# Layer-norm statistics by ScalarE passes, register loads in three parts, and another order in the set-up, in a one-core image kernel

## The reference

```python
x = x + warp(x, fside, angle)            # rigid transform, bilinear gather from the image itself
x = x + ffn(x, expert)                   # relu(x wi^T + low-rank parts) wo^T + low-rank parts,
                                         # low-rank: common ones and those of one of 8 experts per image
x = x + pool(x, prompt)                  # scores tanh(x W1 + b1) v, masked softmax, weighted mean
x = x + norm(x + adapter(x, language))   # adapter: relu(x W1 + b1) W2 + b2, of one of 10 languages
# norm: mean and variance over the 512 columns of each row, then
# (v - mean) * rsqrt(var + 1e-5) * gamma[language] + beta[language]
```

## Time and profile before

| | |
|---|---|
| median of 3 runs | 2290.92 us (2283.33 to 2296.32) |
| profiled execution | 2310.93 us, span 2309.2 us |
| TensorE busy | 2053.8 us, 89%, 15230 instructions |
| VectorE busy | 1970.5 us, 85%, 6602 instructions |
| ScalarE busy | 872.6 us, 38%, 2292 instructions |
| GpSimd busy | 899.9 us, 39%, 1066 instructions |
| chain that ended last | VectorE 44%, TensorE 35%, issue 14%, VectorE's queue 5% |
| mean granted clock of TensorE | 0.959 |

### The profile page before, as it was taken

One profiled execution on the slowest core, in us unless ns is written; L12 is line 12 of the kernel. 1 busy time (PEld: TensorE's weight loads), 2 busy tenths in 40 slices (PEclk: granted clock), 3 DMA queues, 4 the chain that ended last, 5 costly groups with the idle time before them and its releaser, 6 DMA issues.

```text
span 2309.2 us, 53802 instructions
## 1 busy us (share of the span) xinstructions
PE 2053.8 (89%) x15230; PEld 1441.0 (62%) x15230; DVE 1970.5 (85%) x6602; ACT 872.6 (38%) x2292; POOL 899.9 (39%) x1066
## 2 busy tenths in 40 slices
PE   4648999999899999999999899899989999999996
PEld 2336666666666666666666666666666666676673
DVE  7878999988889898889888898898988898899943
ACT  2423433434333343343334334343433433344431
POOL 6224554334434433424333443443344343344201
PEclk8869999999999999999999999999999999999997
DMA  8955465556546555545655655555565456554322
GB/s 233 217 139 129 106 150 136 133 124 153 131 101 142 128 127 137 140 124 110 139 130 123 153 126 137 111 137 132 123 152 133 125 116 139 130 129 122 103 72 64
DMA packets 336209, 303.61 MB, mean 131 GB/s; under 512 B 187010, under 2 KB 255692, under 8 KB 335482
## 3 DMA queue, kind: packets, MB, share of 16 engines
q1 hardware_dynamic: 290074, 184.03, 33.2%
q0 software_dynamic: 42624, 109.35, 19.9%
q10 hardware_dynamic: 3168, 6.29, 1.0%
HBM read 273.71 MB, written 65.70 MB: 147 GB/s over the span
## 4 chain that ended last, share of the span: by engine, by line
DVE 44%; PE 35%; issue 14%; DVEq 5%; SPq 1%; ACT 1%; another core or an unknown queue 1%; DMA 0%; POOL 0%; POOLq 0%; ACTq 0%
DVE work L869 16%; PE bank L1360 12%; PE bank L1398 10%; DVE work L882 3%; DVE work L883 3%; DVE work L881 3%; DVEq L865 2%; PE bank L1216 2%; DVEq L854 2%; PE bank L1292 2%; PE bank L1392 2%; PE bank L1318 2%; DVE warp_sum L896 2%; DVE work L825 2%; DVE hidden_parts L929 1%
## 5 line engine op out<-in xcount | busy, mean ns | idle before, releaser
L1360 PE MATMUL bank<-x1T,wiT 128*128 128x256 f16 x6144 | 768.7, 276 | 22.0 <-issue 21.3
L1398 PE MATMUL bank<-woT,hidden_parts 128*128 128x512 f16 x3072 | 755.9, 383 | 0.0
L869 DVE TENSOR_TENSOR work<-work 128x72 f32<-128x72 f32 x4096 | 682.6, 283 | 58.2 <-issue 50.8
L1360 PEld LDWEIGHTS bank<-x1T,wiT 128*128 128x128 f16 x6144 | 603.8, 99 | 174.8 <-issue 74.5
L592 POOL DMA_INDIRECT work<-strips,gather_now x512 | 627.0, 1225 | 158.9 <-issue 136.4
L1184 ACT ACTIVATE hidden<-bank 128x256 f32<-128x256 f32 x512 | 196.4, 384 | 786.9 <-PE bank L1367 460.2
L1398 PEld LDWEIGHTS bank<-woT,hidden_parts 128*128 128x128 f16 x3072 | 281.8, 99 | 247.2 <-issue 9.8
L588 POOL TENSOR_TENSOR gather_now<-group_now,no_offset 128x8 int32<-128x8 int32 x64 | 30.5, 476 | 874.9 <-DVE work L869 863.3
L929 DVE TENSOR_TENSOR hidden_parts<-hidden,hidden_parts 128x512 f16<-128x512 f32 x256 | 176.6, 690 | 29.3 <-ACT hidden_parts L1186 13.6
L1392 PE MATMUL bank<-hidden_parts,experts 128*128 128x128 f16 x2048 | 200.8, 221 | 0.0
L1186 ACT ACTIVATE hidden_parts<-bank 128x256 f16<-128x256 f32 x512 | 195.4, 382 | 0.0
(11 more groups left out here) (198 smaller groups left out, 2401.0 us busy)
## 6 DMA issues: line engine op xcount, KB each, us to landing
strips<-in_x_dram SPq DMA_DIRECT2D x64, 532.0 KB
lw<-in_L_cond_W_dram SPq DMA_DIRECT2D x128, 256.0 KB
xs<-in_x_dram SPq DMA_DIRECT2D x64, 256.0 KB, 2.7
experts<-ib_dram SPq DMA_DIRECT2D x64, 256.0 KB
gamma_b<-in_L_cond_gamma_dram SPq DMA_DIRECT2D x64, 256.0 KB
x<-in_L_cond_beta_dram POOLq DMA_DIRECT2D x64, 256.0 KB, 6.2
out_dram<-y SPq DMA_DIRECT2D x64, 256.0 KB, 2.5
work<-strips,gather_now POOLq DMA_INDIRECT x512
```

Source lines behind the costliest of these rows:

```text
L869: last = v.tensor_tensor(prods[:, :, :, j, :, row].rearrange("p a b g -> p g b a"), seen, wx.unsqueeze(2).broadcast_to([128, NG, TAPS, TAP ...
L1360: t.matmul(b[:, 0:2 * T], wiT[:, ws, m, tile(f)], x1T[:, xs_, m, :], start=(m == 0 and ws + xs_ == 0), stop=False)
L1398: last = t.matmul(down_ps[k][:, :], hidden_parts[:, hs, f % RING, k * T:(k + 1) * T], woT[:, ws, f, :], start=(first and n == 0), stop=False)
```

## The change

The change has four parts. (1) Mean and variance of the rows of `y` are no longer taken by VectorE's two instructions. ScalarE makes three passes for each image (`moments`): the sum of the row (a copy with an accumulator, into an unused part of `experts`), its mean with a minus sign, and the sum of the squares of `y` minus the mean. `moments(0)` stands behind the last slice of the step, ahead of the two copies of the transposed image; `moments(1)` behind them, ahead of the low part of the ffn's output. VectorE's `centre` waits for the squares and multiplies as before. (2) `sums` loads the 32 registers by three instructions, of 12 behind L882, 12 behind L883 and 8 behind L892. (3) SyncE publishes the input experts first and loads pair 0's, in front of the pixel rows of pair 2's image 0; the output experts are published one image later, behind the strips of image 1. (4) Eight of VectorE's low jobs stand ahead of the wait for the small inputs, four behind, and five more go to step -1; the first hats follow 16 jobs instead of 21.

```diff
+        unread = experts[:, cuts_now[-1]:cuts_now[-1] + 8 * D].bitcast(fp32).rearrange("p (k n d) -> p k n d", k=2, n=2)
...
-            def publish_experts():
+            def publish_inputs():
                 sp.wait_ge(ev_dve, splits[at_job[("ewib", 3)] + 1])
                 sp.dma_start(ia_dram..., ia_all...).then_inc(inputs_out, 16)
+                for c in range(2):
+                    for e in range(E):
+                        sp.dma_start(ib_dram[e, c]..., ib_all[e * R:(e + 1) * R, :]...).then_inc(inputs_out, 16)
+                sp.wait_ge(inputs_out, 16 * (1 + 2 * E))
+
+            def publish_outputs():
                 sp.dma_start(oa_dram..., oa_all...).then_inc(experts_out, 16)
                 for c in range(4):
                     for e in range(E):
                         sp.dma_start(ob_dram[e, c], ob_all[e * R:(e + 1) * R, :]).then_inc(experts_out, 16)
-                (the 16 input experts' stores)
-                sp.wait_ge(experts_out, 16 * (2 + 6 * E))
+                sp.wait_ge(experts_out, 16 * (1 + 4 * E))
...
                         load_strips(i + 3, k, 1 - q)
-                        if isinstance(i, int) and i == -1 and k == 1:
-                            publish_experts()
-                            load_expert_in(0)
+                        if isinstance(i, int) and i == -1:
+                            if k == 0:
+                                publish_inputs()
+                                load_expert_in(0)
+                            else:
+                                publish_outputs()
                         load_pix(i + 3, k, 1 - q)
...
             v.tensor_copy(pix_offs, a4).then_inc(set_ready, 1)
+            evacuate_low(8)
             dve.wait_ge(small_in, 16 * SMALL)
...
-            evacuate_low(17)
+            evacuate_low(4)
...
                     link(v.tensor_tensor(total, total, by_column_tap[:, 1], ALU.add))
-                    link(v.tensor_tensor(total, total, by_column_tap[:, 2], ALU.add))
+                    count[0] += 1
+                    v.tensor_tensor(total, total, by_column_tap[:, 2], ALU.add).then_inc(dve_chain, 1)
+                    if then is not None:
+                        load_offsets(then, 0, 12)
+                    dve.wait_ge(dve_chain, count[0])
                     v.tensor_tensor(total, total, tap_rows[:, 0, :, half], ALU.mult).then_inc(taps_used, 1)
                     if then is not None:
-                        load_offsets(then, 0)
+                        load_offsets(then, 12, 24)
...
                     v.tensor_tensor(warp_sum[:, half], total[:, 0], total[:, 1], ALU.add).then_inc(dve_chain, 1)
                     if then is not None:
-                        load_offsets(then, 1)
+                        load_offsets(then, 24, HALF)
...
-                def statistics(b, k):
+                def centre(b, k):
                     yk = y[:, k, :]
-                    dve.wait_ge(adapt_read, b * 2 + (k + 1))
-                    link(v.bn_stats(stats[:, k, :], yk))
-                    link(v.bn_aggr(mv[:, k, :], stats[:, k, :]))
+                    dve.wait_ge(squares, b * 2 + (k + 1))
                     dve.wait_ge(lang_in[k], b * 48 + 48)
-                    link(v.scalar_tensor_tensor(yk, yk, mv[:, k, 0:1], gamma_b[:, k, :], ALU.subtract, ALU.mult))
+                    link(v.scalar_tensor_tensor(yk, yk, neg_mean[:, k:k + 1], gamma_b[:, k, :], ALU.add, ALU.mult))
...
-                    link(v.tensor_scalar(var_eps[:, :], mv[:, :, 1], EPS, None, ALU.add))
+                    link(v.tensor_scalar(var_eps[:, :], square_sum[:, :], 1.0 / D, EPS, ALU.mult, ALU.add))
...
-            hats_after = {21: [(0, 0, 0), (0, 0, 1)], 27: [(0, 1, 0)], 35: [(0, 1, 1)], splits[-1]: [(1, 0, 0)]}
+            hats_after = {16: [(0, 0, 0), (0, 0, 1)], 27: [(0, 1, 0)], 35: [(0, 1, 1)], splits[-1]: [(1, 0, 0)]}
...
+                def moments(k):
+                    n = c * 2 + k
+                    act.wait_ge(adapt_read, n + 1)
+                    s.activation(unread[:, k, 0, :], y[:, k, :], ACT.Identity, accum_out=row_total[:, k:k + 1]).then_inc(totals, 1)
+                    act.wait_ge(totals, n + 1)
+                    s.activation(neg_mean[:, k:k + 1], row_total[:, k:k + 1], ACT.Copy, scale=-1.0 / D).then_inc(means, 1)
+                    act.wait_ge(means, n + 1)
+                    s.activation(unread[:, k, 1, :], y[:, k, :], ACT.Square, bias=neg_mean[:, k:k + 1],
+                                 accum_out=square_sum[:, k:k + 1]).then_inc(squares, 1)
...
+                if tail:
+                    moments(0)
                 if warp:
                     (the two copies of the transposed image, L1196)
+                if tail:
+                    moments(1)
                 if ffn:
                     project(low_o, low_ps, low_o_ps, low_o_hi)
```

More of the change, by code:

```diff
@@ L153, in build @@
         stats = sb("stats", [T, 2, 6])
-        mv = sb("mv", [T, 2, 2])
+        row_total = sb("row_total", [T, 2])
+        neg_mean = sb("neg_mean", [T, 2])
+        square_sum = sb("square_sum", [T, 2])
         rstd = sb("rstd", [T, 2])
@@ L257, in build @@
         adapt_read = sem("adapt_read")
+        totals = sem("totals")
+        means = sem("means")
+        squares = sem("squares")
         guess_ready = sem("guess_ready")
@@ L265, in build @@
         experts_out = sem("experts_out")
+        inputs_out = sem("inputs_out")
         expert_i_in = sem("expert_i_in")
@@ L421, in load_x @@
                 sp.dma_start(xs[:, q, k, :], x[bass.ds(a * 2 + k, 1)].squeeze(0)).then_inc(x_in[k], 16)
-            def publish_experts():
+            def publish_inputs():
                 sp.wait_ge(ev_dve, splits[at_job[("ewib", 3)] + 1])
-                sp.dma_start(ia_dram.rearrange("e p n -> p e n"), ia_all.rearrange("p (e n) -> p e n", e=E)).then_inc(experts_out, 16)
+                sp.dma_start(ia_dram.rearrange("e p n -> p e n"), ia_all.rearrange("p (e n) -> p e n", e=E)).then_inc(inputs_out, 16)
+                for c in range(2):
+                    for e in range(E):
+                        sp.dma_start(ib_dram[e, c].rearrange("s r f -> r s f"),
+                                     ib_all[e * R:(e + 1) * R, :].rearrange("p (s f) -> p s f", s=2)).then_inc(inputs_out, 16)
+                sp.wait_ge(inputs_out, 16 * (1 + 2 * E))
+            def publish_outputs():
                 sp.dma_start(oa_dram.rearrange("e p n -> p e n"), oa_all.rearrange("p (e n) -> p e n", e=E)).then_inc(experts_out, 16)
@@ L848, in take_offsets, with load_offsets @@
                     v.tensor_copy(offs_now[:, :], offs[:, 2 * par + k, :]).then_inc(dve_chain, 1)
[L850 to L854, removed]
+                def load_offsets(h, start, end):
+                    v.load(regs[start:end], offs_now[0:1, h * HALF + start:h * HALF + end])
                 def products(k, h, start, end, w=w):
@@ L995, in body @@
                         dve.wait_ge(dve_chain, count[0])
-                        for part in range(2):
-                            load_offsets(0, part)
+                        for start in range(0, HALF, HALF // 2):
+                            load_offsets(0, start, start + HALF // 2)
                         products(0, 0, 0, 16)
@@ L1003, in body @@
                     if there(i, 2):
-                        statistics(i - 2, 1)
+                        centre(i - 2, 1)
                     if tail:
@@ L1064, in body @@
                 if tail:
-                    statistics(c, 0)
+                    centre(c, 0)
                 if ahead:
```

## The result

| | before | changed |
|---|---|---|
| median of 5 runs | 2294.18 us (2283.33 to 2296.32) | 2234.12 us (2220.31 to 2248.76) |
| profiled execution | 2310.93 us, span 2309.2 | 2248.76 us, span 2247.1 |
| ratio, 95% interval | | 0.9723 [0.969, 0.9756] |

The kernel is 2.8% faster, 60 us by the medians; predicted were 79 us off the profiled execution, 2212 us as the median, a ratio of 0.966, and 2178 to 2252 as the range. The profiled execution is the slowest of its five. Run and profiled once more, beside other runs of the kernel before (median 2286.37), the same kernel gave 2208.86 us (2202.70 to 2219.17), 0.9675 [0.9653, 0.9697], with a span of 2201.0 us. The two sets of five don't overlap.

The account below looks back on a forecast made before the run. The prediction took TensorE and VectorE waiting for each other in a ring as the bound. Steps 60, set-up 18 and end 1 us made 79 off the profiled 2310.9: 2232, scaled by 0.9913 to a median of 2212 us; range 2178 to 2252.

Parts of the forecast that it names:

- VectorE's saving: Statistics and shorter register-load gaps on VectorE: 1.9 and 1.5 us a step, 3.4 together, 105 over 31 steps.
- Passes: ScalarE's three statistics passes take 1.9 us per image and lie under other work.
- Rival 3: ScalarE's passes for image 1 delay the low copies TensorE needs, ending slower: 2331 us at 8 us of passes; chance 0.03.
- Rival 4: Squares need their own function set, reloaded around each step's tanh: up to 40 us lost, 2252 us; chance 0.04.
- The steps: The 31 steps between first feed-forward matmuls: 45 us saved over 23 steps, 1.95 each, 60 us in all.
- pooled product: TensorE's wait ahead of the second pooled product: 0.37 us a step less, 8.5 of 61.5 us over 23 steps.
- transposes, L1245: TensorE's wait ahead of the warped image's transposes: two sums, 0.74 us, less; some 9.5 of 21 us over 23 steps.
- low halves, L1389 and L1396: TensorE's waits at the slices of `up`, put down to VectorE's late low half: 12 us gone over 23 steps.
- rest, clock above all: Shorter stops leave TensorE's granted clock at full after most of about 8 stops over 2 us: 15 us over 23 steps.
- Rival 1: VectorE's relief passes to the clock of steps in full: 105 + 20 = 125 us, so 2167 us; chance 0.15.
- Set-up: Input experts first and low jobs moved: first feed-forward stage starts 18 us earlier, near 130; bounds 8.8 and 20.
- the ring: Bounding cycle: TensorE's scores, VectorE's masks, loop jump, 32 products and sums, pooled sum, TensorE's second half; steps of 66.6 us.

Follow-up runs that it names:

- the publication alone: Only the order of publication changed (inputs published and pair 0's input experts loaded first, outputs after), low jobs as before, on the kernel before: 0.9979, 2295.70 us.
- the four single parts: Statistics by ScalarE, register loads of 12, 12 and 8, the set-up, or only its publication order, each put alone on the kernel before: 0.9902, 0.9907, 0.9945, 0.9979.
- the eight later profiles: Changed kernel again (0.9675) and seven variants: passes left out, operation added ahead of or behind masks, longer passes, VectorE's loop of four, jump moved, no loop (0.9355 to 0.9927).
- part 3: Only the set-up changed, inputs published first and low jobs in the other order, on the kernel before: 0.9945, 2293.43 us.
- the seven variants of the changed kernel: Changed kernel with passes left out, an operation added ahead of or behind masks, longer passes, VectorE's loop of four, jump moved, or no loop: 0.9355 to 0.9927.

## Why the prediction held, step by step

The forecast of 2212 us lies between the kernel's two medians, 2234.12 and 2208.86; its ratio, 0.966, is under both measured ones, 0.9723 and 0.9675, and near the second. That it comes so near there is in part luck: two terms were off in opposite directions, as told below. The steps:

**VectorE's saving: right.** Statistics: predicted 56 us of busy time, measured 55.2. Loads: predicted 8 and 5 us of idle time left, measured 9.1 and 4.6, so 1.45 us a step for 1.5. They are a little shorter than my line made them: the medians of the two sizes are 848 and 594 ns, for 879 and 659. With 1098 for sixteen that is 63 ns for each register, on about 90 ns. So 12 registers have more room behind 958 ns than I gave them. The Trainium skill ("DMA: Bandwidth & Descriptors", section "Latency and other measured facts") gives a tensor load a floor of about 600 ns. From eight registers up the rows don't go against it; the one load that lies under it is that of a single register, 274 ns on SyncE's queue, and loads of fewer than eight on VectorE's queue were not run.

**Passes: right.** 1.8 us for 1.9, and leaving them out changes nothing. ScalarE's busy time rose by 107.9 us and not 125, since my 1.9 us held three waits of 0.05, which are not busy time, and the reads take 191 and 186 ns for 207. Rival 3 is real but far off: by the estimate above the cover is 4.7 us where I had 4.2, so the 79 us would have been eaten by passes of 7.2 us where I had 6.7.

**Rival 4: false.** Two function loads in all: squares came with the set in use, and tanh and exp did not have to be loaded again. The Trainium skill ("ScalarE: Activation LUTs", section "Table sets: the hidden batching unit") leaves square out of the functions that it names for every set; here it ran with the set that tanh and exp use, and no run shows more than that.

**The steps: 60 us predicted, 48.4 measured in the profile on record, 66.0 between two nearly undisturbed profiles** (the publication alone, whose steps are those of before, 2042.3, against the second of the changed kernel, 1976.3). By terms, added up stop by stop from TensorE's timeline over the same 24 steps (5 to 28). The first pair is the profile before and the first one of the changed kernel, the second pair the two of the heading; the forecast is scaled from 23 steps:

| term, us in 24 steps | predicted | first pair | second pair |
|---|---|---|---|
| pooled product | 8.9 | 62.3 - 46.3 = 16.0 | 62.8 - 46.1 = 16.7 |
| transposes, L1245 | 9.9 | 27.9 - 22.4 = 5.5 | 18.5 - 12.0 = 6.5 |
| low halves, L1389 and L1396 | 12.5 | 27.6 - 24.2 = 3.4 | 22.6 - 9.1 = 13.5 |
| rest, clock above all | 15.7 | 11.1 | 15.6 |
| all | 47 | 1620.7 - 1584.7 = 36.0 | 1602.3 - 1550.0 = 52.3 |

In the first pair the term that was mis-sized most is the third, 3.4 us for 12.5: I had put L1360's 19.7 us down to a late low half, and in the profile on record 21.3 us were still there, 9.1 in the second. In the first VectorE stands still seven times for 2.1 to 3.8 us between the two pooled sums, released by nothing of this core, and TensorE has small gaps in the same steps:

```profile
543.87 0.75 DVE L974 SCALAR_TENSOR_TENSOR x<-bank,pool_scale,x 128x512 f32<-128x512 f32 x1 [3.63 <-remote]
```

The second profile has none, and its even steps, but for those behind TensorE's jump, come at 61.5 us where the first has 62.3 to 67.1; the whole difference is 2014.0 - 1976.3 = 37.7 us. The kernel before has six of them on record, of 1.9 to 2.7 us, the four single parts 4, 8, 7 and 2; the eight later profiles none. All but two (at 231 and 239 us, in step 1, with part 3 and with the publication alone) lie in looped steps, and these all in even ones, ahead of the second pooled sum, so at one place of the loop's list. The same kernel has seven and none, so its list alone doesn't decide. Nor do single executions explain it all, as I had expected: the medians of the two sets of five differ by 25 us, those of the kernel before beside them by 8, and the ranges of the two sets don't meet. The single parts ran on one chip, the other eight on two further ones, so the runs don't tell whether the chip, the hour or where the program lies in memory decides. A late supply of instructions would fit; it was not tried by itself.

The transposes' term was too large, by 3.4 us in the second pair: two sums' 0.74 us do not come off in full, and some 0.9 us are left even in quiet steps. The pooled product's was too small by 7 to 8: the stops in odd steps stay, as predicted, but at 3.73 us for 4.6 where I gave 0.37 for the one sum, and those of 0.64 in even steps, which I had not told apart, fell to 0.15. One error stands against the other.

**Rival 1 was limited by more than I named.** In the looped steps the wait for the second scores grew from 0.9 at most to between 1.1 and 1.4 us, not to the 2 that I had named as a sign. Not only the wait for the scores keeps VectorE's 3.4 us from passing in full: in even steps TensorE is full at 61.5 us, 2.2 below before. I never worked out this floor, though the busy row of TensorE gave it.

**Set-up: 18 us predicted, 13.8 in the first profile, 17.7 in the second** (130.94; I had 130.5). In the seven variants of the changed kernel it starts at 130.4 to 133.2. SyncE's issues are as planned: the 16 input stores now come ahead, and take 15.25 us for 10.00. The late load of the output experts, which I had put at nothing, shows no stop of TensorE between 130 and 200 us.

```profile
92.39 15.25 SPq L436 DMA_DIRECT2D ib_dram<-experts  x16
...
114.73 0.55 SPq L457 DMA_DIRECT2D experts<-ib_dram  x1
```

VectorE sets the start, as I had it: its first product was forecast at 65.9 and came at 70.47, then 67.12. The eight low jobs fill the idle time. In the first profile ScalarE then stood 5.87 us, with TensorE's transposes there, and VectorE's next low job behind it; in the second the four jobs run together:

```profile
58.25 1.28 DVE L681 SCALAR_TENSOR_TENSOR wiT<-bank,wiT 128x512 f16<-128x512 f32 x2
64.13 0.69 DVE L681 SCALAR_TENSOR_TENSOR wiT<-bank,wiT 128x512 f16<-128x512 f32 x1 [4.61 <-issue]
...
70.47 1.71 DVE L882 TENSOR_TENSOR work<-work 128x72 f32<-128x72 f32 x10 [2.75 <-issue]
```

```profile
57.70 2.47 DVE L681 SCALAR_TENSOR_TENSOR wiT<-bank,wiT 128x512 f16<-128x512 f32 x4
60.50 1.43 DVE L840 TENSOR_TENSOR work<-group_now,frac_pix 128x256 f32<-128x256 f32 x4 [0.32 <-DMA offs<-offs_dram]
...
67.12 5.12 DVE L882 TENSOR_TENSOR work<-work 128x72 f32<-128x72 f32 x32 [5.03 <-issue]
```

So the term held, and of the 4 us short of it in the first profile most are one stand-still. **Tail:** 1 us predicted, 0 measured in the first profile; from the last start of L1438 to the end it takes 98.2 us before, 98.3 and 93.8 in the two profiles, and 98.3 to 101.8 with the single parts, so one us can't be told there.

## What to carry to other kernels

Find the ring first, and the point in it behind which an engine has no room: here one operation of 0.9 us cost 0.2% ahead of VectorE's second masks and 2.5% behind them, and dropping the loop's jump, which is no part of the change, gained 71 us more. A loop's jump belongs where its engine would wait anyway. And before a saving on one engine is given in full, work out the other's floor in one undisturbed step. Two profiles of one kernel can differ by 38 us in the same steps, so take a second one before a small term is read from the first.

## What the hardware showed that I had not expected

- VectorE's jump, 2.9 us between masks and products (20.50 against 17.58), costs 71 us in 12 jumps, 5.9 for each. TensorE's stop grows with it, and behind the stop the granted clock falls from 2.4 to 1.2 GHz.
- A straight list with VectorE's 6474 counted instructions shows no gap over 0.2 us from 420 to 1960 us that is put down to "issue".
- Register loads on VectorE's queue take 63 ns more for each register: 594, 848 and 1098 ns for 8, 12 and 16. One register on SyncE's queue took 274, more than that line gives (153).
- The 16 stores of input experts took SyncE 10.00 us in the kernel before and, in the place that they have now, 12.01 (part 3 alone), 13.62 and 15.25 us (the changed kernel's two profiles); 32 stores took 18.25. So the place alone doesn't set it; what does was not looked into.
